# Sorted token rows of the routed experts: transposes moved from TensorE to quadrant loads and a VectorE block transpose

## The reference, cut to what matters

```python
scores_aE = x_aD @ router_DE
vals_aK, idx_aK = jax.lax.top_k(scores_aE, 1)
gates_Ea = jax.nn.sigmoid(masked_aE).T
routed_in_EaD = gates_Ea[:, :, None] * x_aD[None, :, :]
mid_EaF = silu(einsum('ead,edf->eaf', routed_in_EaD, w1_eDF)) * einsum('ead,edf->eaf', routed_in_EaD, w3_eDF)
routed_out_EaD = einsum('eaf,efd->ead', mid_EaF, w2_eFD)
shared_aD = silu(x_aD @ ws1_DF) * (x_aD @ ws3_DF) @ ws2_FD
out_aD = shared_aD + routed_out_EaD.sum(axis=0)
```

## Time and profile before

| what | value |
|---|---|
| median of 3 runs | 703.83 us |
| the profiled execution's own time | 700.68 us |
| its span | 698.9 us |
| TensorE busy | 681.9 us (98%) |
| VectorE, ScalarE, GpSimd busy | 466.9, 439.4, 245.3 us |
| mean granted TensorE clock | 0.999 |

### The profile page before, as it was taken

The page is one execution under the profiler, slowest core; times in us unless marked ns, Lnnn a source line. Parts: engine busy times, 40 slices in busy tenths (PEclk is TensorE's granted clock), DMA queues, the critical chain, the costliest instruction groups (busy, mean ns, idle before and its releaser), DMA issues. The chain is left out here.

```text
span 698.9 us, 17942 instructions
## 1 busy us (share of the span) xinstructions
PE 681.9 (98%) x5977; PEld 632.5 (90%) x5978; DVE 466.9 (67%) x960; ACT 439.4 (63%) x1208; POOL 245.3 (35%) x375
## 2 busy tenths in 40 slices
PE   7899999999999999999999999999999999999997
PEld 7789989999899998998988978898889999999997
DVE  5778778887877877888778676366645665333333
ACT  4788887887878888788787774342334654232232
POOL 5823213232232321322445541058140453424233
PEclk9999999999999999999999999999999999999999
DMA  8454545544454454454445534003557997677660
GB/s 294 126 141 123 144 130 141 137 133 137 128 154 123 132 150 130 137 137 130 142 134 131 148 82 130 0 1 103 160 182 250 351 335 252 255 243 274 222 260 8
DMA packets 65273, 111.67 MB, mean 160 GB/s; under 512 B 13900, under 2 KB 41806, under 8 KB 62544
## 3 DMA queue, kind: packets, MB, share of 16 engines
q1 hardware_dynamic: 55136, 93.67, 43.5%
q0 software_dynamic: 7072, 14.71, 7.2%
q10 hardware_dynamic: 3024, 2.76, 1.2%
HBM read 63.74 MB, written 16.67 MB: 115 GB/s over the span
## 5 line engine op out<-in xcount | busy, mean ns | idle before, releaser
L946 PE MATMUL PS<-BIG 128*128 128x256 f32 (+1 forms) x1164 | 195.9, 322 | 1.8 <-DVE BIG L773 1.8
L946 PEld LDWEIGHTS PS<-BIG 128*128 128x128 f32 x1164 | 166.1, 190 | 16.1 <-DVE BIG L773 1.8
L620 ACT ACTIVATE PR<-PS,NMX 128x256 f32<-128x256 f32 x256 | 117.8, 476 | 4.4 <-DVE NMX L779 4.4
L1933 PE MATMUL PS<-XST,W 128*128 128x128 f32 x1012 | 116.8, 275 | 0.0
L1933 PEld LDWEIGHTS PS<-XST,W 128*128 128x128 f32 x1012 | 114.9, 192 | 0.1
L629 ACT ACTIVATE PR<-PR,RINV 128x256 f32<-128x256 f32 x256 | 106.0, 519 | 0.0
L791 DVE STREAM_TRANSPOSE PR<-PR 128x512 f32<-128x512 f32 x124 | 80.4, 684 | 3.0 <-ACT PR L629 2.2
L475 POOL DMA_DIRECT2D PT<-PR x128 | 64.6, 510 | 50.6 <-DVE PR L791 43.1
L779 DVE TENSOR_REDUCE NMX<-PS 128x4 f32<-128x1024 f32 x64 | 75.5, 1197 | 1.2 <-PE PS L1004 1.2
L966 PE MATMUL PS<-KVF,WQ 128*128 128x128 f32 x512 | 65.6, 281 | 1.6 <-DVE KVF L752 1.0
L966 PEld LDWEIGHTS PS<-KVF,WQ 128*128 128x128 f32 x512 | 59.6, 192 | 7.0 <-issue 5.0
(11 more groups left out here) (185 smaller groups left out, 1150.6 us busy)
## 6 DMA issues: line engine op xcount, KB each, us to landing
W<-in_w SPq DMA_DIRECT2D x21, 1408.0 KB, 6.2
PT<-PR SPq DMA_DIRECT2D x368, 64.0 KB, 2.1
PT<-PR POOLq DMA_DIRECT2D x128, 64.0 KB, 2.5
W<-in_w SPq DMA_DIRECT2D x8, 640.0 KB, 5.6
turned<-CXN SPq DMA_DIRECT2D x15, 256.0 KB, 2.0
INT<-turned SPq DMA_DIRECT2D x60, 64.0 KB, 2.0
xs_sorted<-C SPq DMA_DIRECT2D x26, 128.5 KB, 3.2
W<-in_w SPq DMA_DIRECT2D x8, 352.0 KB, 3.4
```

Source lines behind the costliest of these rows:

```text
L620: last = act.activation(probs, logits, ACT.Exp, bias=NMX[:, g, own, p % 2:p % 2 + 1], accum_out=SUM[:, p, own:own + 1])
L946: last = pe.matmul(dst, stat(s, k), mov(m, k), start=n == 0, stop=n == len(todo) - 1)
L1933: last = pe.matmul(h[:, P * c:P * (c + 1)], lhs13(W13[par], k, c), XST[par][:, k, :], start=k == 0, stop=k == KD - 1)
```

## The change

- `XS` now holds a tile as [128, 4, 64]: quadrant j (partitions 32j to 32j + 31) takes features 64j to 64j + 63 of all 128 rows, as four blocks of 32 rows side by side. That takes four DMAs per tile (`load_rows`) with runs of 64 numbers (256 bytes), in place of one with runs of 257.
- One VectorE block transpose of 128 x 256 (`turn_rows`) turns each 32 x 32 block over into `XST`. Features then stand on the partitions in another order, and the host gives the routed W1 and W3 rows in that order.
- TensorE's `ex` and ScalarE's `copy_x` are gone. VectorE gets `turn_rows(t + 2)` behind `gate_lo(t)`; tile 0's stands in the last shared group after `hidden` of slice 4, tile 1's after that group.
- The token numbers of all 23 tiles come in one DMA of single numbers into `WHOF`, converted by one VectorE copy; GpSimd waits for it once.
- ScalarE issues four loads for tile t + 3 at the head of `routed_act(t)`; tile 1's, then the token numbers', in the last shared group between SiLU and high half of slice 4; tile 2's ahead of `w2_hi(0)`. SyncE issues only tile 0's.

```diff
-        XS = [sb(f"XS{i}", [128, DI]) for i in range(2)]
...
+        XS = [sb(f"XS{i}", [128, 4, 2 * 32]) for i in range(2)]
+        WHOF = sb("WHOF", [128, NT])
         WHO = sb("WHO", [128, NT], I32)
-        XST = [sb(f"XST{i}", [128, KD, P]) for i in range(2)]
+        XST = [sb(f"XST{i}", [128, 4, KD, 32]) for i in range(2)]
         SIL = sb("SIL", [128, FT * P])
...
-        def tile_rows(t, n):
-            return t[n * P:(n + 1) * P, :] if isinstance(n, int) else t[bass.ds(n * P, P), :]
+        def load_rows(engine, t, par):
...
+            rows = xs[t * P:(t + 1) * P, :] if isinstance(t, int) else xs[bass.ds(t * P, P), :]
+            rows = rows.rearrange("(i b) f -> b i f", i=4)
+            for j in range(4):
+                engine.dma_start(XS[par][32 * j:32 * (j + 1), :, :], rows[:, :, 64 * j:64 * (j + 1)]).then_inc(d_xs[par], 16)
...
             sp.wait_ge(d_sc, 16 * NB)
-            for t in range(2):
-                sp.dma_start(XS[t][:, :], tile_rows(xs, t)).then_inc(d_xs[t], 16)
+            load_rows(sp, 0, 0)
             load_output(2)
...
             def gather_base(t):
-                pool.wait_ge(a_who, t + 1)
+                if t == 0:
+                    pool.wait_ge(v_who, 1)
                 if t >= 2:
...
                     if last and f == FT - 2:
-                        copy_x(0, 0, free=False)
+                        act.wait_ge(d_sc, 16 * NB)
+                        load_rows(act, 1, 1)
+                        act.dma_start(WHOF[:, :], xs[0:NT * P, D:DI].rearrange("(t p) a -> p (t a)", p=P),
+                                      allow_slow_non_contiguous=True).then_inc(d_who, 16)
                     shared_mid(g, f)
...
-            def copy_x(t, par, free=True, load=True):
...
-                act.wait_ge(t_ex, t + 1)
-                if free:
-                    act.wait_ge(t_eh, t - 1)
-                act.activation(XST[par][:, :, :], PS[:, EY[par], D:D + KD * P].rearrange("p (k q) -> p k q", k=KD),
-                               ACT.Copy).then_inc(a_ex, 1)
-                act.activation(WHO[:, t:t + 1] if isinstance(t, int) else WHO[:, bass.ds(t, 1)],
-                               XS[par][:, D:DI], ACT.Copy).then_inc(a_who, 1)
-                if load:
-                    act.wait_ge(a_who, t + 1)
-                    act.dma_start(XS[par][:, :], tile_rows(xs, t + 2)).then_inc(d_xs[par], 16)
...
-            def routed_act(t, par, copy_next):
...
-                if copy_next:
-                    copy_x(t + 1, 1 - par, free=not (isinstance(t, int) and t == 0),
-                           load=not (isinstance(t, int) and t + 3 >= NT))
+            def rows_ahead(t, par):
+                act.wait_ge(v_xst, t - 1)
+                load_rows(act, t, par)
...
+            def routed_act(t, par):
...
+                if not (isinstance(t, int) and t + 3 >= NT):
+                    rows_ahead(t + 3, 1 - par)
                 act.wait_ge(t_eh, t + 1)
...
                 shared_group(g, gate=g == 1, last=g == NG - 1)
+            rows_ahead(2, 0)
             w2_hi(0)
             for t in range(NE - 1):
-                routed_act(t, t % 2, True)
+                routed_act(t, t % 2)
             with act.Fori((NE - 2) // 2, (NT - 5) // 2) as i:
-                routed_act(2 * i + 1, 1, True)
-                routed_act(2 * i + 2, 0, True)
-            routed_act(NT - 4, 1, True)
-            routed_act(NT - 3, 0, True)
-            routed_act(NT - 2, 1, True)
+                routed_act(2 * i + 1, 1)
+                routed_act(2 * i + 2, 0)
+            routed_act(NT - 4, 1)
+            routed_act(NT - 3, 0)
+            routed_act(NT - 2, 1)
             last_act(NT - 1, 0)
...
-            def shared_group(g, route=False, number=False):
+            def turn_rows(t, par):
+                dve.wait_ge(d_xs[par], 64 * (t // 2 + 1) if isinstance(t, int) else 32 * (t - par) + 64)
+                if not (isinstance(t, int) and t < 2):
+                    dve.wait_ge(t_eh, t - 1)
+                dve.transpose(XST[par][:, :, :, :].rearrange("p i k q -> p (i k q)"),
+                              XS[par][:, :, :].rearrange("p i f -> p (i f)")).then_inc(v_xst, 1)
...
+            def shared_group(g, route=False, number=False, last=False):
                 for f in range(2):
...
                     hidden(g, f)
+                    if last and f == FT - 2:
+                        turn_rows(0, 0)
                     if route and f == 2:
...
             for g in range(1, NG):
-                shared_group(g, route=g == 1, number=g == 2)
+                shared_group(g, route=g == 1, number=g == 2, last=g == NG - 1)
+            turn_rows(1, 1)
             def gate_hidden(t, par):
...
                 gate_lo(t, par)
+                if not (isinstance(t, int) and t + 2 >= NT):
+                    turn_rows(t + 2, par)
                 if isinstance(t, int) and t + 1 < NE:
...
                 add_shared(NG - 1, q, OUTB_LAST)
+            turn_rows(2, 0)
             w2_lo(1)
+            dve.wait_ge(d_who, 16)
+            dve.tensor_copy(WHO[:, :], WHOF[:, :]).then_inc(v_who, 1)
...
             gate_lo(1, 1)
+            turn_rows(3, 1)
             w2_lo(2)
...
                 for q in range(4):
-                    if banks is OUTB_LAST and q == 1:
-                        pe.wait_ge(a_ex, 2)
                     if q == 2 and ranks:
...
-            def shared_group(g, ranks=False, last=False):
+            def shared_group(g, ranks=False):
                 if GT // P * (g + 1) > AHEAD:
...
                 for f in range(2, FT):
-                    if last and f == FT - 1:
-                        ex(0, 0)
                     shared_hidden(g, f)
...
-            def ex(t, par):
...
-                pe.wait_ge(d_xs[par], 16 * (t // 2 + 1) if isinstance(t, int) else 8 * (t - par) + 16)
-                if isinstance(t, int) and t == 0:
-                    pe.wait_ge(v_mid, FT * NG - 2)
-                else:
-                    pe.wait_ge(a_ex, t)
-                if isinstance(t, int) and t == 3:
-                    pe.wait_ge(v_so, TOK // P)
-                elif not isinstance(t, int) or t >= 4:
-                    pe.wait_ge(v_ey, t - 3)
-                for k in range(KD):
-                    last = pe.transpose(PS[:, EY[par], D + P * k:D + P * (k + 1)], XS[par][:, 128 * k:128 * (k + 1)], IDENT[:, :])
-                last.then_inc(t_ex, 1)
...
-                pe.wait_ge(a_ex, t + 1)
+                pe.wait_ge(v_xst, t + 1)
                 pe.wait_ge(d_w13[par], 64 + 16 * (t // 2) if isinstance(t, int) else 8 * (t - par) + 64)
...
                     for k in range(KD):
-                        last = pe.matmul(h[:, P * c:P * (c + 1)], lhs13(W13[par], k, c), XST[par][:, k, :],
+                        last = pe.matmul(h[:, P * c:P * (c + 1)], lhs13(W13[par], k, c), XST[par][:, :, k, :],
                                          start=k == 0, stop=k == KD - 1)
...
-                pe.wait_ge(a_ex, min(t + 3, NT) if isinstance(t, int) else t + 3)
+                if isinstance(t, int) and t == 1:
+                    pe.wait_ge(v_so, TOK // P)
+                elif not isinstance(t, int) or t > 1:
+                    pe.wait_ge(v_ey, t - 1)
                 mid = (MRH[par], MRL[par])
...
-            def routed(t, par, following=True):
-                if following:
-                    ex(t + 1, 1 - par)
+            def routed(t, par):
                 eh(t, par)
...
             for g in range(1, NG):
-                shared_group(g, ranks=g == 1, last=g == NG - 1)
+                shared_group(g, ranks=g == 1)
             pe.wait_ge(v_so, 4 * (NG - 1))
...
             eh(0, 0)
-            ex(1, 1)
             shared_out(NG - 1, OUTB_LAST)
...
             routed(NT - 2, 1)
-            routed(NT - 1, 0, following=False)
+            routed(NT - 1, 0)
             ey(NT - 1, 0)
...
         "wq_t": np.asarray(L0_xcond_Wq).T[features], "wkv_t": np.asarray(L0_xcond_Wkv).T[features], "wo_t": np.asarray(L0_xcond_Wo).T,
-        "router": L0_ffn_router_DE, "w13": hidden_columns(L0_ffn_w1_eDF, L0_ffn_w3_eDF), "w2": w2, "w2_last": w2_last,
+        "router": L0_ffn_router_DE, "w13": hidden_columns(*(np.asarray(w)[:, features] for w in (L0_ffn_w1_eDF, L0_ffn_w3_eDF))), "w2": w2, "w2_last": w2_last,
         "ws13": hidden_columns(L0_ffn_ws1_DF, L0_ffn_ws3_DF), "ws2": ws2, "ws2_last": ws2_last,
```

More of the change, by code:

```diff
@@ L1288, in experts_part @@
         d_bs = sem("d_bs")
-        a_who = sem("a_who")
+        d_who = sem("d_who")
+        v_who = sem("v_who")
         p_zero = sem("p_zero")
@@ L1298, in experts_part @@
         d_y = [sem(f"d_y{i}") for i in range(2)]
-        t_ex = sem("t_ex")
-        a_ex = sem("a_ex")
+        v_xst = sem("v_xst")
         t_eh = sem("t_eh")
```

## The result

The changed kernel takes 705.83 us (median of 21 runs, 703.85 to 711.62); the kernel before, run beside it, 704.14 us (21 runs, 703.07 to 705.49). The ratio is 1.0035, with a 95% interval of [1.0022, 1.0048]: slower by 2.5 us, or by 1.7 in the medians. The profiled execution took 704.33 us, 1.5 us less than the median, so what follows reads one of the quicker executions.

A forecast was written before the change was run, and what follows sets the result against it. The prediction took TensorE, busy 98% of the span, as the bound. Transposes -4.3, handover +2.0 and late weights +0.4 summed to -1.9 us, from 703.83 to 701.9 us; range 699.4 to 707.0.

The forecast's parts named there:

- Part 1: TensorE, routed tiles: removing twenty pairs of transposes at 0.217 us each gains 4.3 us.
- part 4: DMA queues, tiles 3 to 7: smaller row packets make weights late, a stall of 0.4 us, between 0 and 1.8.
- Part 2: VectorE's block transpose takes 0.4 us a tile behind `gate_lo`, beside `eh`, and costs nothing.
- Part 3: Handover from the shared expert: ScalarE's added load issues start `eh(1)` 2.0 us later, between 0.7 and 2.8.
- the bounds that I had named: Sign at the handover: the prediction is wrong if `eh(1)` starts outside 536.4 to 538.5 us.
- The rival of the numbers' load: ScalarE's queue: 2,944 single numbers block the next issue for 7.1 us, giving 705.8 us; chance 0.28.

The follow-up runs named there:

- e1: Changed kernel with the load of token numbers moved from ScalarE to SyncE, behind the three base stores; ratio 1.0011 to the kernel before.
- e2: Changed kernel with SyncE waiting for the last low half before it issues the base stores; ratio 1.0046 to the kernel before.
- e3: Changed kernel with the same four row loads a tile in 128 runs of 1 KB, routed output values differing; ratio 1.0057 to the kernel before.
- e4: Changed kernel with SyncE issuing the rows of tiles 1 to 3 and the numbers, ScalarE none before tile 4's; ratio 1.0043 to the kernel before.
- e11: Kernel before with each row load that ScalarE issues cut into four DMAs, bytes and values unchanged; ratio 1.0045 to the kernel before.
- e9: Changed kernel with one row DMA a tile instead of four, 128 runs of 1 KB, routed output values differing; ratio 0.9959 to the kernel before.
- e5: The changed kernel run again, unchanged; ratio 1.0038 to the kernel before.
- e13: The kernel before, run and profiled again unchanged; ratio 0.9995.
- e6: Changed kernel with ScalarE's four loads for tile t + 3 moved from the head of `routed_act(t)` to behind `SiLU(t)`; ratio 1.0020 to the kernel before.
- e8: Changed kernel with all row loads and the numbers issued by SyncE, tile t + 1's rows behind tile t's weights; ratio 0.9991 to the kernel before.

## Why the prediction was wrong

**The forecast** was -1.9 us, the measurement is +2.5 (1.7 in the medians), inside the range and on the other side of zero.

**Part 1, right.** Given 20 x 0.217 = 4.3 us. Measured 3.3 between `eh(1)` and the last `eh`, with 1.4 us of stalls in it (part 4): 4.7, as a tile takes 6.90 us and not 6.92. The moving operand in pieces of 32 columns costs nothing: `eh` took 4.91 us as in the earlier trace rows.

**Part 2, right.** The transpose takes 0.43 to 0.45 us, forecast 0.4, beside `eh`:

```profile
561.00 0.45 DVE L1710 STREAM_TRANSPOSE XST<-XS 128x256 f32<-128x256 f32 x1
```

**Part 3 is the step that failed**, in two places. The first is one figure, "a burst of four costs 2.0 (between 1.7 ... and 2.2)". I had taken it from two quiet bursts of SyncE. Tile 1's burst took 4.23 us, with the numbers' issue 5.1 instead of 2.5, in the place behind SyncE's three base stores (issued 522.90 to 525.39); bursts ahead of those stores took 1.95 to 2.01 (e1, e2, e3). The last low halves came late by that, which made a stall of 1.58 us that my working doesn't have: I let `shared_out` start without a wait. The 1.7 us inside it, which I did forecast, came as 1.62, and the 0.3 to 0.5 ahead of `eh(0)` as 0.68. So 3.8 us instead of 2.0; `eh(1)` stood outside the bounds that I had named. The trace of before had the warning, in the earlier trace rows: an issue beside other traffic took 2.44 us in place of 0.47. I used it for a rival alone, and not as the upper bound of a burst.

The second is "Later on, the bursts cost nothing: they end before the SiLU for which ScalarE waited up to 4.4 us". I took the wait of before as room for the burst, and left out that a burst can't start before `turn_rows`, which stands behind `gate_lo` of the tile before. That closes the loop described above. In after's own profile it costs nothing from tile 8 on (82.8 us); in e1, e2 and e4, which have the same code there, it cost 2.9 to 3.5 us. In the first tiles the three added issues cost 0.9 us in e11, and e9 with one issue needs 49.3 us where after needs 49.7.

**Part 4, sized nearly right.** The packets of the row loads took 19 ns each (forecast 18, though the slope that I named gives 16): in 562 to 580 us they held 9.3% of 16 engines for 1,414 packets. Late weights cost 1.2 us at tile 6, and with three rounds of 6.97 us 1.4 in all (forecast 0.4, between 0 and 1.8): W13 was issued at 568.70, `eh(6)` started at 578.42. e3 shows that the size of the packets is not the reason for the loss: with long runs the ratio is no lower.

```profile
578.42 3.81 PE L1931 MATMUL PS<-XST,W 128*128 128x128 f32 x32 [1.01 <-issue]
```

**The sum by measured terms** is -4.7 + 3.8 + 1.4 = +0.5 us; the table's wholes give 168.3 - 167.8 = +0.5 too. The measured +1.7 (medians) to +2.5 (ratio) is more, and e5's whole is even 0.3 us below e13's, so 1.2 to 2.0 us are in no profile of the changed kernel. Both of its profiles caught quick executions, 1.5 and 3.2 us under the median. The loop would fill the gap: it costs 2.9 us in e1, whose profile took its median time, and the kernel with the burst out of the loop spreads less (e6 704.9 to 709.0 us, e5 704.6 to 710.7). That the slower executions of the changed kernel, up to 711.6 us, run in this loop is likely; no profile of it shows one, so that stays open.

**The rival of the numbers' load** gave 705.8, the time that was measured, but by another way: it had 7.1 us of blocking behind that load. With the load off ScalarE the ratio is 1.0011 against 1.0035, and the burst behind it took 3.62 us there, 2.44 in after, not 7.1. In e9 ScalarE's queue moved 3,392 packets between 520 and 536 us: three row loads of 128 + 16, and 2,960 = 2,944 + 16 for the numbers. The Trainium skill's page "DMA: Bandwidth & Descriptors" (Rules for kernel authors) says that a last dimension which isn't contiguous becomes one descriptor per element; the trace agrees, with one packet for each of the 2,944 numbers. They landed 5.2 us after an issue of 0.91 in after.

## What to carry to other kernels

The count of DMAs that a compute engine issues is a cost of its own: cutting one load into four, with bytes and values unchanged, cost 0.45% here, and four issues against one, with equal bytes, differed by 1% (e3 and e9, on two chips). Before adding issues in front of work that others wait for, see what they themselves wait for: where that is the end of the tile before, they lengthen a loop over all engines, and an engine's idle time in the old profile isn't room for them. Take their duration from a stretch in which another engine is issuing and the DMA engines are full, not from a quiet one. Moving the issues to an idle queue only helps if what stands behind them in that queue isn't needed soon.

## What the runs showed of the hardware that was not expected

- **An issue takes longer beside and behind other DMAs.** Four row loads took 1.95 to 2.01 us on ScalarE ahead of SyncE's base stores (e1, e2, e3), 4.23 beside and behind them (after), and 3.62 behind a load of 2,944 single numbers that SyncE had issued (e1). Within SyncE's own queue it was the same: 0.46 us each for the first eight loads in e8 and 1.03 each for the four behind the numbers.

```profile
518.93 3.67 SPq L1329 DMA_DIRECT2D XS<-xs_sorted  x8
...
530.10 0.57 SPq L1393 DMA_DIRECT2D WHOF<-xs_sorted  x1
530.72 4.13 SPq L1329 DMA_DIRECT2D XS<-xs_sorted  x4
```

The Trainium skill's page "Perfetto Trace Analysis" (DMA Instruction — HWDGE (DVE, Sync)) says that a descriptor generator is locked for exclusive use while a DMA's descriptors are made, and that the issue's recorded time includes the wait for the lock. That can be in after's burst, whose second issue took 1.28 us beside SyncE's last store (to 525.39), but it can't be all of it: the last two took 2.49 us from 525.49 on, when SyncE issued nothing and the 16 DMA engines were full (share 1.10 in 526 to 528 us). Full engines alone don't do it either: at a share of 0.96 in 552 to 554 us a burst took 1.77. What makes an issue slow isn't separated by these runs.

```profile
524.18 1.28 ACTq L1329 DMA_DIRECT2D XS<-xs_sorted  x1
525.49 2.49 ACTq L1329 DMA_DIRECT2D XS<-xs_sorted  x2
```

The Trainium skill's page "DMA: Bandwidth & Descriptors" (Issuing engines are not separate DMA queues) says that issuing from several engines saves only the sequencer's time, usually small beside the DMA. Here that time was not small: four issues instead of one made about 1% of the kernel (e3 against e9, on two chips).

- **Four issues a tile cost time on SyncE's queue too.** In e8 `eh(1)` started as early as in e9 (14.5 us after slice 4 in both), but tiles 1 to 8 took 52.3 us instead of 49.3. SyncE issued tile 3's rows up to 534.85, tile 2's weights at 537.41, 13.3 us after slice 4 (e9: 11.5), and the last base store (512 KB) close behind, at 539.32; the gather could start 9.3 us later (e9: 7.6; before: 5.6, 535.98 to 541.62). The stretch 537 to 541 us of e8 (columns as in e4) has full engines; in e9 the shares of this stretch and the next are 0.93 and 0.67, in e8 0.96 and 0.93:

```profile
537.00:541.00 4.00, 4.00 (x37) 4.00 (x36) 2.39 (x5) 0.00 (x0) 0.00 (x0) 1.00 0.96 297
```

- **The same program gave two profiles 6.1 us apart**, all of it in two late releases in the shared expert. They stand in eleven of the sixteen profiles, and in none of the four kernels (e1 to e4) that ran on the first experiments' chip. Two profiles should be compared from a common event next to the change, not from the span's start. What releases late there is open.
